# Two moves of work in a fused two-layer kernel: the linear attention's numerators into the routing, the second attention's first row maxima into the projection before it

## The reference, cut to what matters

```python
x = L0_attn_x                                   # (2, 2048, 256), float32
xn = layernorm(x)
s = linear_attention(xn, W_qkv, W_out)          # num = q_feat @ kv, den = max(q_feat @ k_sum, 1e-6), num/den @ W_out
g = silu(block(xn))                             # causal softmax attention, then 8 experts, top 2, capacity 1024
x = x + s * g
xn = layernorm(x)
s = causal_attention(xn, Wq, Wk, Wv) @ Wo       # 16 heads of 32 columns, softmax with the row maximum taken off
g = silu(int4_linear(xn) + lora(xn))
x = x + s * g
```

## Time and profile before

| | us |
|---|---|
| median of 3 executions (lowest, highest) | 3025.88 (3023.87, 3026.47) |
| the profiled execution: its own time | 3017.3 |
| its span (first to last instruction) | 3015.5 |
| routing, 1136 to 1181 | 45 |
| numerators and output of the linear attention, 1645.6 to 1700.0 | 54.4 |
| the eight blocks of the projection, 1700.0 to 1907.9 | 207.9 |
| second attention, from 1911.6 to the span's end | 1103.9 |

### The profile page before, as it was taken

How to read it: one execution, slowest core, us unless ns; L and a number is a source line. 1 busy time by engine, 2 the same in 40 slices (tenths; PEclk the granted TensorE clock), 3 DMA queues, 4 the chain that set the end, 5 groups by cost and what they waited for, 6 DMA issues and landing times. The chain is left out here.

```text
span 3015.5 us, 46320 instructions
## 1 busy us (share of the span) xinstructions
PE 2836.4 (94%) x18017; PEld 1315.2 (44%) x18017; DVE 2016.5 (67%) x4387; ACT 1540.1 (51%) x2565; POOL 985.5 (33%) x529
## 2 busy tenths in 40 slices
PE   7998999999999973999999999899999999999999
PEld 4664333333333342676666645323333333333327
DVE  7887889999999844000001765688887877878823
ACT  3552467776767764222221444345565565566571
POOL 1000000110111103121100430157777777777791
PEclk9997799999999996999999999789999999999999
DMA  4322121233213124222110466212020220202103
GB/s 130 96 77 76 34 49 35 48 62 62 48 26 62 27 58 139 65 74 87 60 49 28 149 189 193 74 35 62 9 64 12 67 64 8 64 12 67 67 12 119
DMA packets 140923, 200.57 MB, mean 67 GB/s; under 512 B 14320, under 2 KB 107520, under 8 KB 137616
## 3 DMA queue, kind: packets, MB, share of 16 engines
q1 hardware_dynamic: 130288, 173.00, 20.7%
q0 software_dynamic: 9056, 24.59, 3.9%
q10 hardware_dynamic: 1360, 0.01, 0.0%
HBM read 121.01 MB, written 76.02 MB: 65 GB/s over the span
## 5 line engine op out<-in xcount | busy, mean ns | idle before, releaser
L940 ACT ACTIVATE at_probs<-at_st 128x512 f32<-128x512 f32 (+3 forms) x1280 | 588.4, 542 | 442.5 <-PE at_st L1034 283.8
L903 POOL TENSOR_TENSOR at_probs<-at_probs 128x2048 f32<-128x2048 f32 (+3 forms) x205 | 725.9, 3546 | 214.3 <-ACT at_probs L940 135.8
L387 DVE TENSOR_REDUCE at_part<-at_s 128x1 f32<-128x512 f32 (+3 forms) x1280 | 689.3, 601 | 68.5 <-PE at_s L425 33.0
L362 ACT ACTIVATE at_probs<-at_st 128x1024 f32<-128x1024 f32 (+3 forms) x640 | 541.8, 895 | 279.9 <-PE at_st L444 144.4
L966 DVE TENSOR_REDUCE at_part<-at_s 128x1 f32<-128x512 f32 x768 | 498.3, 682 | 68.8 <-PE at_s L1026 65.0
L960 DVE CUSTOM_DVE_ANT_0 at_s<-at_s,at_later 128x384 f32<-128x384 f32 (+3 forms) x512 | 246.6, 497 | 103.9 <-PE at_s L1026 102.6
L504 PE MATMUL at_acc<-at_probs,at_v 128*32 128x512 f32 (+3 forms) x2560 | 308.3, 556 | 8.1 <-ACT at_otile L349 7.8
L2319 DVE TENSOR_TENSOR ex_ot<-ex_bank,lin_b 128x512 f32<-128x512 f32 x32 | 22.1, 692 | 439.1 <-PE ex_bank L2349 439.1
L1858 POOL DMA_DIRECT2D att_sums<-att x28 | 14.7, 529 | 757.0 <-DMA att<-at_otile 757.0
L2292 ACT ACTIVATE ex_hT<-ex_bank,ex_b 128x512 f32<-128x512 f32 x128 | 87.9, 687 | 334.5 <-PE ex_bank L2339 334.5
L2339 PE MATMUL ex_bank<-ex_xT,lin_w 128*128 128x512 f32 x512 | 225.2, 598 | 1.0 <-ACT ex_xT L2285 1.0
(11 more groups left out here) (340 smaller groups left out, 3941.9 us busy)
## 6 DMA issues: line engine op xcount, KB each, us to landing
att<-at_otile SPq DMA_DIRECT2D x64, 256.0 KB, 2.1
lin_w<-in_W SPq DMA_DIRECT2D x16, 1024.0 KB, 7.7
at_v<-v SPq DMA_DIRECT2D x11, 1024.0 KB, 11.9
v<-pr_vt SPq DMA_DIRECT2D x32, 256.0 KB
exp_out<-ex_ot SPq DMA_DIRECT2D x32, 256.0 KB, 2.1
v<-p_vt SPq DMA_DIRECT2D x32, 256.0 KB, 3.7
p_xs<-in_x SPq DMA_DIRECT2D x8, 512.0 KB, 5.0
qhi<-p_parts SPq DMA_DIRECT2D x8, 512.0 KB, 3.3
```

Source lines behind the costliest of these rows:

```text
L362: act.activation(probs[:, quad % RING, heads_down * p:heads_down * (p + 1), off:QB], st_ps[n % st_slots][:, :, off:QB], ACT.Exp, scale=EXP ...
L387: dve.tensor_reduce(part[:, w % 2, qt * HG + h, j:j + 1], s_ps[n % S_SLOTS][:, 0:width], AX.X, ALU.max).then_inc(item_free, 1)
L903: pool.tensor_tensor(total, total, probs[:, slots.slot[quad], :, off:QB], ALU.add).then_inc(add_done, 1)
L940: act.activation(probs[:, slots.slot[quad], h, off:QB], st_ps[n % ST_SLOTS][:, off:QB], ACT.Exp, scale=EXP_SCALE).then_inc(exp_done, 1)
```

## The change

1. The numerators move from the projection's loop to `route`. The product with the mask of heads moves to POOL, at the start of the first attention's POOL program, with the mask loaded by a DMA there. In `route` PE makes the 16 pairs of products into three PSUM tiles, nine pairs ahead of the counts, and ACT copies each pair's numerators over `mix` and the denominators to `den`, with a token tile's normalisation ahead of every second pair. The last of the four chunks of token numbers goes from ACT to DVE. In `experts` DVE divides all of `mix` by the denominators before its first result. The loop of pairs in the projection keeps the transposition and the product with `W_out`; the gathers are released by the transpositions.
2. The S of the first two units (of 32) are made in the last projection, in pairs of heads, at most two tiles behind a job of blocks 5, 6 and 7, in the same three PSUM tiles; DVE's maxima, shifts and strips stand behind them in its program. SP writes the strips' rows behind the outputs of blocks 6 and 7. The second attention starts with the S of its third unit and the ST of the first, and its loads of group 1 are issued at its start.

```diff
 (narrow_attention, POOL)
+            pool.wait_ge(heads_ld, 16)
+            for n in range(B * NF):
+                pool.tensor_tensor(kvd[:, n, :], kv_sum[:, n, :], kvd[:, n, :], ALU.mult).then_inc(kv_ready, 1)
...
+EARLY = 2
+EARLY_TILES = [(u, qt, h, j) for u in range(EARLY) for qt in range(4) for h in range(0, HG, 2) for j in range(u + 1)]
+EARLY_SLOTS = [(slot, b) for b, slots in ((5, "kB kB vA vA vB vB T y"), (6, "qB qB kB kB vA vA vB vB T y"),
+                                          (7, "qB qB kB kB vA vA")) for slot in slots.split()]
+EARLY_TURN = {("qA", 6): 0, ("vB", 7): 1}
 (wide_schedule)
-    for unit in units:
+    for unit in units[EARLY:]:
 (route, ACT)
-            for t in range(NT - 8, NT):
-                normalise_rows(act, t, x_all, shift, rstd, z, z_ready, z_kept)
-            for n in range(0, SLOTS, CHUNK):
+            for m in range(PAIRS):
+                if m % 2 == 0:
+                    normalise_rows(act, NT - 8 + m // 2, x_all, shift, rstd, z, z_ready, z_kept)
+                both = num_ps[m % BANKS][:, :, 0:NF * WID].rearrange("p t (c n) -> p t c n", c=NF)
+                act.wait_ge(num_ready, m + 1)
+                act.activation(mix[:, 2 * m:2 * m + 2, :, :], both[:, :, :, 0:P], ACT.Copy).then_inc(num_kept, 1)
+                act.activation(den[:, 2 * m:2 * m + 2, :, :], both[:, :, :, P:WID], ACT.Copy).then_inc(num_kept, 1)
+            for n in range(0, SLOTS - CHUNK, CHUNK):
 (route, DVE)
+            dve.wait_ge(equal_ready, SLOTS // CHUNK)
+            tt(tokens[:, last, :], equal[:, last, :],
+               token[:, NT - CHUNK:NT].unsqueeze(2).to_broadcast([P, CHUNK, WIDE]), ALU.mult).then_inc(last_tokens, 1)
 (route, PE)
-            counts()
+            def numerator(m):
+                if m >= BANKS:
+                    pe.wait_ge(num_kept, 2 * (m - BANKS + 1))
...
+            for m in range(PAIRS):
+                numerator(m)
+                if m == 8:
+                    counts()
 (experts, DVE)
+            dve.tensor_scalar(flat, flat, FLOOR, None, ALU.max).then_inc(bounded, 1)
+            dve.reciprocal(flat, flat).then_inc(inverted, 1)
+            for n in range(0, NT, 4):
...
+                dve.tensor_tensor(heads, heads, by, ALU.mult).then_inc(divided, 1)
 (combine_and_project, DVE)
-            for m in range(PAIRS):
-                normalise(m)
...
+            def maxima(i):
+                u, qt, h, j = EARLY_TILES[i]
+                width = QB if j < u else (qt + 1) * P
+                pe_s.wait(dve, f"S {i}")
...
+                if j < u:
+                    last = dve.tensor_reduce(part[:, u, row:row + 2, j:j + 1], tile[:, :, 0:width], AX.X, ALU.max)
+                else:
+                    for y in range(2):
+                        last = dve.tensor_tensor_reduce(...)
 (combine_and_project, PE)
-                if m < PAIRS:
-                    numerator(m)
...
+            def early(s, b):
+                for i in EARLY_AT.get((s, b), ()):
+                    u, qt, h, j = EARLY_TILES[i]
+                    width = QB if j < u else (qt + 1) * P
+                    d = banks.take(pe, f"S {i}")
+                    for y in range(2):
+                        mm = pe.matmul(d[:, y, 0:width], carried.q[0:96, h + y, u * QB + qt * P:u * QB + (qt + 1) * P],
+                                       carried.k[0:96, h + y, j * QB:j * QB + width], start=True, stop=True)
 (wide_attention)
+                        if place_of[ev[1]] < EARLY:
+                            pe.wait_ge(carried.row_ld, 16 * HG * EARLY)
```

More of the change, by code:

```diff
@@ L230, with narrow_attention @@
 FIRST_LOADS = (12 + HG) * 16
-def narrow_attention(nc, tag, C, q_hi, q_lo, k_hi, k_lo, v, out, q_first, k_first, first_ld, masks, A):
+def narrow_attention(nc, tag, C, q_hi, q_lo, k_hi, k_lo, v, out, q_first, k_first, first_ld, masks, A, heads, kv_sum, kvd):
     hd = 16
@@ L2392, in combine_and_project, with early_jobs @@
             jobs.append((f"s {m - 2}", "act", f"s {m - 2}"))
+    def early_jobs(at):
+        for i in EARLY_AT.get(at, ()):
+            pe_names.append(f"S {i}")
+            jobs.append((f"S {i}", "dve", f"max {i}"))
+        if at in EARLY_TURN:
+            u = EARLY_TURN[at]
+            pe_names.append(f"row {u}")
+            jobs.append((f"row {u}", "dve", f"strip {u}"))
     for b in range(NB):
@@ new lines, in shifts @@
+            def shifts(u):
+                dve_s.wait(dve, f"max {EARLY_LAST[u]}")
+                link(dve.tensor_reduce(rowmax[:, u, :], part[:, u, :, 0:u + 1], AX.X, ALU.max))
+                link(dve.tensor_scalar(shift[:, u, :, 0], rowmax[:, u, :], -1.0 / MSHIFT, None, ALU.mult))
+                step(f"shift {u}", stt(out=shift[:, u, :, 1], in0=rowmax[:, u, :], scalar=-1.0 / MSHIFT,
+                                       in1=shift[:, u, :, 0], op0=ALU.mult, op1=ALU.subtract))
+            def early(s, b):
+                for i in EARLY_AT.get((s, b), ()):
+                    maxima(i)
+                    if i in EARLY_LAST:
+                        shifts(EARLY_LAST.index(i))
+                if (s, b) in EARLY_TURN:
+                    u = EARLY_TURN[s, b]
+                    pe_s.wait(dve, f"row {u}")
+                    step(f"strip {u}", dve.tensor_copy(strip[:, u, :],
+                                                       banks.tile(f"row {u}")[0:2 * HG, 0, 0:QB // 2].bitcast(F16)))
@@ L2707, in _ @@
                 lower(1, "k", "B", b)
+                for s in ("kB", "vA", "vB", "T"):
+                    early(s, b)
                 pe_s.wait(dve, f"y {b}")
@@ L2777, in _ @@
                         step(f"{s}{half} {b}", mm)
+                        early(f"{s}{half}", b)
                 for half in "AB":
```

201 lines of the change are left out of this document (121 added, 80 removed).

## The result

The changed kernel takes **3040.15 us** (median of 12 runs, 3027.53 to 3047.36), the kernel before beside it 3026.11 us (12 runs, 3020.58 to 3033.58): a ratio of 1.0041, 95% interval 1.0027 to 1.0054. It is 12 us slower; 3006 and "faster" had been forecast. The profiled execution took 3040.62 us, its span is 3038.9 (3015.5 before).

What follows compares the result with a forecast made beforehand. PE was taken as the bound, busy 94% of the span, with idle seams. Terms -13 (loop), -1 (routing), +26 (blocks) and -32 (attention) summed to -20 us, from 3025.88 to 3006 us; range 2991 to 3020.

Steps and rivals of the forecast that it cites:

- Part 1b: Routing: PE makes nine pairs ahead of the counts, two cold, then full clock; last products start 1 us earlier.
- rival B: Routing stays at 1.2 GHz: stage 9 us longer instead of 1 shorter, total -10, 3016 us; chance 0.12.
- 3.2 us of dense work: Earlier loop of pairs: after 3.9 us idle, products ran at clock 0.50 this long, then at 1.00.
- Part 1a: Projection's loop of pairs: numerators leave, 16 x 0.92 = 14.7 us, 1.7 given back: -13 us (-10 to -15).
- Part 2a: Projection's blocks 5 to 7: early S cost 8.3 us of matmuls, 16.6 of waits, about 1 for strips: +26 us.
- Part 2b: Second attention's start: unit 2's first ST comes after 38.1 us instead of 70.5: -32 us (-24 to -38).
- C: Second attention: only the matmuls' own work leaves, gain 8 instead of 32; total +4, 3030 us; chance 0.08.
- D: Projection: waits drop the clock, blocks 6 and 7 run at 1.2 GHz; total +21, 3047 us; chance 0.05.

Runs made afterwards that it cites:

- e1: The change's first part alone (numerators moved, no early S, attention loads as before) against the kernel before: 2998.94 us, ratio 0.9948.
- e10: The change with early S spaced, strip ahead of group 2's load and gathers paced up to token tile 12: 2997.55 us, ratio 0.9911 against the kernel before.
- e11: The change with gathers paced up to token tile 12 and nothing else: 3028.55 us, ratio 1.0006 against the kernel before.
- e13: e10 with the later blocks' gathers spread out too: 2993.91 us, ratio 0.9931 against the kernel before.
- e17: e13 again, unaltered, in another session: 2997.11 us, ratio 0.9942 against the kernel before.
- e3: The change with group 2's 4 MB load issued after the strip of group 1's first unit: 3006.30 us, ratio 0.9973 against the kernel before.
- e4: The change once more, unaltered: 3043.06 us, ratio 1.0051 against the kernel before.
- e15: The change unaltered a third time, in another session: 3023.70 us, ratio 1.0033 against the kernel before.
- e2: The kernel before with the early S of units 0 and 1 alone, numerators as before: 3034.29 us, ratio 1.0066.
- e5: The change with the 24 early S pairs placed apart and block 7's combination moved ahead in block 5: 3022.74 us, ratio 0.9997 against the kernel before.
- e6: e5 with the strip issued ahead of group 2's load: 3006.66 us, ratio 0.9927 against the kernel before.
- e12: e1 again, numerators alone with gathers unbroken, in another session: 3017.78 us, ratio 0.9967 against the kernel before.
- e18: e1 once more, numerators alone with gathers unbroken, in another session: 3005.18 us, ratio 0.9959 against the kernel before.
- e14: The kernel before with the gathers of blocks 0 and 1 no longer waiting for each pair's numerators: 3013.55 us, ratio 0.9997.
- e16: e14 again, the kernel before with unbroken gathers, in another session: 3013.84 us, ratio 0.9991.

## Why the prediction was wrong

- **Part 1b, the routing (-1)**: right in the mechanism, 1.8 us too small. The clock did not stay at 1.2 GHz: it was 0.50 to 1136, 0.72 from there to 1138 and 1.00 from 1138 to 1150, with the pairs running, and rival B fell. ("3.2 us of dense work" is read too short: by the earlier trace rows PE had worked since 1645.59, 1.2 us before the window of the earlier trace rows. The sum doesn't hang on it.)
- **Part 1a, the loop (-13)**: the arithmetic was right wherever PE's events came in time (loop 40.5 to 41.8, forecast 41.4). The step that failed is the half sentence "POOL's gathers, no longer waiting for numerators ... make that possible, about 0.5 us early or late". The wait on the numerators had also paced POOL. Without it the gathers ran unbroken, and in four of seven sessions the loop took 51.0 to 57.6 us, which is most or all of the gain lost again. In the other three the gain is there (e1), and with the gathers paced it is there in both kinds (e10, e11, e13, e17). How unbroken gathers hold up PE's events stays open.
- **Part 2a, the blocks (+26)**: eight waits forecast, eight found; their sum is 14.4 us, where 15.0 had been forecast (16.6 with 1.6 of clock). The mis-sized term is the clock: in the change's profile three jobs behind waits of 5.47 and 1.98 us were slow, 5.1 us in all, where one was forecast at 1.6. With the 1.6 us of block 0 that is 5 of the 7 us missing; the other 2 no run took apart. In e3, e4 and e15 only the job behind 5.47 was slow in blocks 5 to 7, and there the blocks took 237.1 to 237.4, still 29 above before. e2's took 234.8, 26.9 above.
- **Part 2b, the attention (-32)**: up to unit 2's first ST 27 us were gained, 43.4 against 38.1 forecast. The step that failed is "From that point on the program is the same, so the gain is 70.5 less what the same point takes now". The planner's order past that point was a new one, with 8 KB behind 4 MB on SP's queue; the wait is 14.9 us and 17 us of the attention's time (e3); e5 and e6 are 16 us apart by it. In the rest some 5 of the 27 are given back as well, which no run took apart.
- **The rivals**: C gave the size of the attention's gain nearly right (-8; it is -4.7), but that is luck, for its mechanism is another: PE was not bound all along, since with the strip first it gained 21.6. D had the sign that came true, but the clock cost 5.1 us in three slow jobs and not half the clock over two blocks. (What the prediction says of matmul groups that cycle through PSUM tiles stands in the Trainium skill, TensorE: Matmul & The Clock Gate, under A second HAM failure mode: psum-queue depth-cycling, the section behind the one that it names. The trace agrees in part: there were falls to half clock behind waits of 1.98 us, but the blocks as a whole ran at 0.97.) That two unseen queue effects could each take a forecast gain whole was in no rival, and the chance for slower, 0.05, was far too small for a change that rearranges two queues.
- **The best version**: numerators moved, S apart, strip first, every gather paced: 21 us faster than before in one session without late events (e13), 17 in another (e17); e10, nearly the same kernel, 27 in a session with them, in which the kernel before was slower too. The numerators alone were 16, 10 and 12 us faster (e1, e12, e18). Beside each other, in one session, e17 was 17 us and e18 12 us faster: everything beyond the numerators brings 5 us there (8 by the medians), and the two intervals overlap.

## What to carry to other kernels

When a change takes out a wait, ask what else that wait spaced out: here it paced POOL's gathers, and in some sessions that was worth as much as the matmuls removed. When a planner writes the order, compare the order of every queue to the program's end, DMA issues of a few KB beside loads of MB above all, before adding up a gain "from that point on the same". In a ring of three PSUM tiles, two short fillers in a row hand the next job the tile of the job that has just ended, whose result is not copied out yet; one filler at a time hands it an older tile. And when runs of several sessions are compared, look whether the kernel before moved between them as well.

## What the runs showed of the hardware

- Events of PE that ACT, SP, POOL and DVE see 2 to 10 us late, two at once at the end of a delay, while POOL issues a software gather each 1.25 us for some 6 us or more. ACT's events were not late (0.05 us to PE, at 1668.70). It came in the profiles of four of seven sessions, on a chip in one session and not in another. What in the chip is held up stays open, and so does whether unbroken gathers do it in the kernel before.
- In the six profiles with the change's order of S (the change, e2, e3, e4, e11, e15) the job behind block 5's wait of 5.1 to 5.5 us was slow each time, for part of it at half clock (5.4 to 6.4 us instead of 3.70); the job behind the twelve waits of 1.98 us twice, both in one profile; behind the six of 1.66 once. Block 0's y products, behind a wait of 2.12 to 2.16 us in all twenty profiles, took 5.3 or 5.4 us in eleven of them and 3.7 in nine, in two profiles of one and the same kernel once each (e14, e16). The waits repeat to 0.04 us (but for e2's 5.12), the clock does not.
- A strip of 8 KB issued 3.8 us behind the first of 4 MB of loads on SP's queue was used 17.2 us after its issue.
